# Reordered steps of a block with windowed attention and routed experts: maxima first on VectorE, values behind the scores, the shared expert in the general banks, the second normalisation and what follows it two steps sooner

## The reference

```
x = x + attention(layernorm(x))
x = x + ffn(layernorm(x))
attention: q, k, v = x Wq^T, x Wk^T, x Wv^T; 16 heads of 8 channels; each query sees
           the 64 keys up to itself (blocks of 64, own and previous); softmax; then Wo^T
ffn:       scores = sigmoid(x G) + bias, 16 experts in 4 groups; the 2 groups with the largest
           sum of their top two; in them the top 4 experts, weights normalised times 2.5
           y = sum over experts of weight * (silu(x Wg) * (x Wu)) Wd, experts of width 64
           + silu(x Sg) * (x Su) Sd, a shared expert of width 128
```

## Time and profile before

| | us |
|---|---|
| median of 3 runs (lowest, highest) | 792.83 (791.32, 793.52) |
| profiled execution | 793.12 |
| its span | 791.3 |
| busy: TensorE, weight loads | 699.4, 563.1 |
| busy: VectorE, ScalarE, GpSimd | 507.4, 541.0, 457.4 |

### The profile page before, as it was taken

How to read it: one execution, slowest core, us unless ns; L and a number is a source line. 1 busy time by engine, 2 the same in 40 slices (tenths; PEclk the granted TensorE clock), 3 DMA queues, 4 the chain that set the end, 5 groups by cost and what they waited for, 6 DMA issues and landing times. The chain is left out here.

```text
span 791.3 us, 19511 instructions
## 1 busy us (share of the span) xinstructions
PE 699.4 (88%) x6256; PEld 563.1 (71%) x6256; DVE 507.4 (64%) x1584; ACT 541.0 (68%) x1603; POOL 457.4 (58%) x564
## 2 busy tenths in 40 slices
PE   3566799998989999898989999898999989998887
PEld 2445577777867778686867777777777878786765
DVE  1556666758676665757676675857666576875454
ACT  3586778686877767687776868687776768763232
POOL 5323256657676675757566675767567575435443
PEclk9998799999999999999999999999999999999899
DMA  5000031220303131130403122030313112131321
GB/s 156 1 28 27 1 97 54 80 84 21 123 22 106 53 104 57 47 114 2 133 27 108 53 84 77 21 123 18 109 50 108 53 53 95 38 113 35 101 95 41
DMA packets 50884, 53.63 MB, mean 68 GB/s; under 512 B 5792, under 2 KB 32032, under 8 KB 50720
## 3 DMA queue, kind: packets, MB, share of 16 engines
q1 hardware_dynamic: 50848, 53.18, 21.2%
HBM read 44.25 MB, written 4.72 MB: 62 GB/s over the span
## 5 line engine op out<-in xcount | busy, mean ns | idle before, releaser
L566 ACT ACTIVATE probs<-PS,neg_max 128x96 f32<-128x96 f32 (+1 forms) x1024 | 244.7, 354 | 80.6 <-DVE neg_max L728 80.3
L455 POOL TENSOR_TENSOR gate<-gate,spread 128x512 f32<-128x512 f32 x128 | 163.6, 1278 | 217.7 <-ACT gate L514 105.7
L694 DVE STREAM_TRANSPOSE probsT<-probs 128x768 f32<-128x768 f32 (+1 forms) x128 | 116.3, 908 | 101.6 <-ACT probs L566 101.6
L718 DVE SCALAR_TENSOR_TENSOR tu<-th,PS 128x512 f32<-128x512 f32 x128 | 87.5, 683 | 108.2 <-PE PS L798 77.2
L980 PE MATMUL PS<-wd,hh 128*128 128x128 f32 x1024 | 139.2, 279 | 6.7 <-DVE OUT L708 4.1
L796 PE MATMUL PS<-x_hi,w_hi 128*128 128x512 f32 x288 | 126.9, 441 | 15.3 <-DVE tu L718 14.4
L980 PEld LDWEIGHTS PS<-wd,hh 128*128 128x128 f32 x1024 | 127.3, 193 | 15.2 <-DVE hh L760 5.4
L467 POOL TENSOR_TENSOR hh<-gate,tu 128x512 f32<-128x512 f32 x100 | 128.4, 1284 | 13.7 <-POOL gate L455 13.4
L530 ACT ACTIVATE th<-PS 128x512 f32<-128x512 f32 x128 | 80.2, 627 | 75.7 <-PE PS L798 75.6
L728 DVE TENSOR_REDUCE neg_max<-PS 128x4 f32<-128x384 f32 (+1 forms) x256 | 122.7, 515 | 12.0 <-PE PS L901 10.5
L798 PE MATMUL PS<-x_lo,w_hi 128*128 128x512 f32 x288 | 115.1, 400 | 0.0
(11 more groups left out here) (102 smaller groups left out, 956.0 us busy)
## 6 DMA issues: line engine op xcount, KB each, us to landing
spread<-weights_by_expert SPq DMA_DIRECT2D x256, 128.0 KB, 2.9
X<-x SPq DMA_DIRECT2D x32, 256.0 KB, 3.1
OUT<-H SPq DMA_DIRECT2D x16, 256.0 KB, 2.9
out<-OUT SPq DMA_DIRECT2D x16, 256.0 KB, 3.0
ffn_stage<-w_gu SPq DMA_DIRECT2D x1, 1152.0 KB, 5.7
wd<-w_down SPq DMA_DIRECT2D x1, 512.0 KB, 6.5
weights_by_expert<-cT SPq DMA_DIRECT2D x16, 32.0 KB, 1.6
probsT<-w_att SPq DMA_DIRECT2D x1, 192.0 KB, 3.0
```

The source lines that it names most:

```text
L455: tt(gate2[:, :], gate[:, k % 2, :], spread[:, k % SP_BUFS, :], ALU.mult).then_inc(s_g2, 1)
L566: ins = nc.scalar.activation(probs[:, u % 2, tt, 2 * rows + e, j0:KW], PS[:, rows, n * KW + j0:n * KW + KW], ACT.Exp, bias=neg_max[:, rows ...
L694: v_.transpose(probsT[:, b, :, t0:t0 + 2, c0:3, :].rearrange("p g t c q -> p t g (c q)"), probs[:, u % 2, :, :, c0 * Q:KW]).then_inc(s_pt, 1)
L718: v_.scalar_tensor_tensor(tu[:, k % 2, :], th[:, :], 1.0, PS[:, 5, :], ALU.add, ALU.mult).then_inc(s_tu, 1)
```

## The change

- Stages: VP and VB one step later; LN2 one step sooner, XT2, LG, RT, CT, FF, DN, YE two steps sooner; SH stays in its step.
- The shared expert's gate and up leave banks 4 and 5 for two uses of the ring (LATE, WEIGHTS), with a tanh tile of its own (`th_s`). QP and CT move to the ring's place POST, LG to WEIGHTS, VP to LATE; the ring has 16 uses a slot.
- Within a step TensorE does FF, SC, CT, then PV, OT, ON, OW, SH, QP, KP, VP, LG, DN, XT2, XT. Before, PV, VP and LG came first and DN last.
- VectorE does `tu`, the two maxima, and after them all else; the turning of the probabilities comes late in the step.
- ScalarE does CT's copy and the shared tanh between the two halves of the exponentials, then OE, XT2, LG, XT, QP, KP, VB.
- GpSimd does both expert products first and LN1 last.
- In slots 0 to 2 (`filling`) the two 64-row halves of SC go one after the other, each with its own wait. TensorE starts with 24 tiny matmuls (`WARM`).

```
-QP, KP, VP, VB = 5, 6, 6, 7
+QP, KP, VP, VB = 5, 6, 7, 8
-LN2 = 17
-XT2 = 19
-LG = 24
-RT = 24
-CT = 27
+LN2 = 16
+XT2 = 17
+LG = 22
+RT = 22
+CT = 25
 SH = 27
-FF = 28
+FF = 26
-DN = 29
-YE = 37
+DN = 27
+YE = 35
 RING = (3, 6)
-EARLY, POST, WEIGHTS, LATE = range(4)
+EARLY, POST, LATE, WEIGHTS = range(4)
-    (EARLY, (VP, LG)), (LATE, (XT, QP, KP, XT2, XT2 + 4)),
-    (POST, (OT, OT + 4, ON, ON + 4, OW, OW + 4)), (WEIGHTS, (CT,)))
+    (LATE, (XT, KP, VP, XT2, XT2 + 4, SH)),
+    (POST, (QP, CT, OT, OT + 4, ON, ON + 4, OW, OW + 4)), (WEIGHTS, (LG, SH)))
+def filling(slot):
+    return slot.fixed and slot.n < 3
...
 @block.scalar, in a step
-LG tanh; FF tanh and copy; ON copy; CT copy; SH tanh; XT copy; XT2 copy; SC; QP; KP; OE; VB
+FF tanh and copy; ON copy
+                    for rows in range(2):
+                        if g:
+                            act.wait_ge(s_m, 2 * (g.n * NU + u) + rows + 1)
...
+                            ins.then_inc(s_p, 1)
+                        if rows == 0:
+                            between_halves()      # CT copy, SH tanh
+OE; XT2; LG; XT; QP; KP; VB
...
 @block.vector, in a step
-TR; VP; YE; LN1; tu; routing; SC maxima with routing between; LN2; OT; OW; hh; SH; XT; XT2
+tu; SC maxima; YE; VP; routing; OT; OW; LN2; LN1; TR; XT2; hh; SH; XT
+                        side, bank = filled(dve, sl, s, LATE)
+                        dve.wait_ge(s_ths, g.n + 1)
+                        v_.scalar_tensor_tensor(fa[:, :], th_s[:, :], 1.0, bank, ALU.add, ALU.mult
+                                                ).then_inc(s_taken[side], 1)
+                        taken(dve, sl, s, LATE)
+                        side, bank = filled(dve, sl, s, WEIGHTS)
+                        ins = v_.scalar_tensor_tensor(hs[:, :], fa[:, :], 0.5, bank, ALU.mult, ALU.mult)
+                        ins.then_inc(s_taken[side], 1)
...
 @block.tensor
+            pe.wait_ge(s_pool, 1)
+            for _ in range(WARM):
+                mm(PS[0:NT, 7, 0:NT], half_neg[:, :], half_neg[:, :], start=True, stop=True)
...
+                        if filling(sl):
+                            for rows in range(2):
+                                if not (g.n == 0 and u == 0):
+                                    pe.wait_ge(s_p, 2 * (g.n * NU + u) + rows - 1)
+                                hide(u, rows)
+                                scores(g, u, rows, 0)
+                                scores(g, u, rows, 1)
+                        else:
+                            pe.wait_ge(s_p, 2 * (g.n * NU + u))
+                            hide(u, 0, 1)
+                            for tt in range(2):
+                                for rows in range(2):
+                                    scores(g, u, rows, tt)
...
+                        for place, n in ((LATE, WG), (WEIGHTS, WU)):
+                            side, bank = free(place)
+                            exact3(bank, *w2(n + P * NP), *x2).then_inc(s_filled[side], 1)
```

More of the change, by code:

```diff
@@ L145 @@
 PREPARE = 4
+WARM = 24
 ORDER_PER_SLOT = 5
@@ L721, in slot @@
-                    routing(sl, s, 3)
                     g, u = at(sl, s, SC, 1, NU)
@@ L809, in gate_up @@
                 x2 = x2_hi[:, g.par, :], x2_lo[:, g.par, :]
[L810 to L816 removed]
+                exact3(PS[:, 4, :], *w2(WG + P * k), *x2).then_inc(s_g, 1)
@@ new lines, in gate_up, with hide @@
+                exact3(PS[:, 5, :], *w2(WU + P * k), *x2).then_inc(s_u, 1)
+            def hide(u, *halves):
+                parts = ((0, 2, 1, 1, 1), (2, 4, 0, 2, 1)) if u % 4 == 0 else ((0, 4, 0, 0, 2),)
+                for n0, n1, which, first, step in parts:
+                    for rows in halves:
+                        r = slice(64 * rows, 64 * rows + 64)
+                        dst = PS[:, rows, 0:4 * KW].rearrange("p (n k) -> p n k", n=4)[:, n0:n1, :]
+                        hidden = slice(first, KW // Q, step)
+                        mm(blocks3(dst)[:, :, hidden, :], ident4[r, :],
+                           blocks2(band[r, which, :])[:, hidden, :].unsqueeze(1).broadcast_to(
+                               [64, n1 - n0, len(range(3)[hidden]), Q]),
+                           start=(n0 == 0), stop=False, skip_group_check=True)
@@ L821, in slot, with free @@
                         pe.wait_ge(s_cst, 2)
+                    def free(place):
+                        use = shared_use(sl, s, place)
+                        if not (sl.fixed and use.before == 0):
+                            pe.wait_ge(s_taken[use.bank], use.before)
+                        return use.bank, PS[:, RING[use.bank], :]
+                    g, k = at(sl, s, FF, 1, NP)
+                    if g:
+                        gate_up(g, k)
+                    g, u = at(sl, s, SC, 1, NU)
+                    if g:
+                        if u == 0:
+                            taken(pe, slot_before(sl), QP % STEPS, POST)
+                            taken(pe, slot_before(sl), KP % STEPS, LATE)
+                        if filling(sl):
[11 more added lines that the diff above has]
+                                    scores(g, u, rows, tt)
+                    g, _ = at(sl, s, CT)
+                    if g:
+                        side, bank = free(POST)
+                        pe.wait_ge(s_cb, g.n + 1)
+                        for n in range(NT):
+                            ins = nc.tensor.transpose(bank[0:E, P * n:P * n + P], comb[:, n, :], ident)
+                        ins.then_inc(s_filled[side], 1)
                     for turn_, stage in enumerate(PV):
@@ L844, in slot @@
                             ins.then_inc(s_o_ps, 1)
-                    def free(place):
-                        use = shared_use(sl, s, place)
-                        if not (sl.fixed and use.before == 0):
-                            pe.wait_ge(s_taken[use.bank], use.before)
-                        return use.bank, PS[:, RING[use.bank], :]
-                    g, _ = at(sl, s, VP)
-                    if g:
-                        side, bank = free(EARLY)
-                        exact3(bank, *w2(WV), xT_hi[:, :], xT_lo[:, :]).then_inc(s_filled[side], 1)
```

334 lines of the change are left out of this document (146 added, 188 removed).

## The result

The changed kernel takes 815.73 us (median of 4 runs, 812.19 to 819.33); the kernel before took 792.08 in the same comparison. The ratio is 1.029 [1.025, 1.033]: slower, where 771.2 and "faster" had been predicted. The profiled execution took 816.72 us, its span 814.9.

What follows compares the result with a forecast made beforehand. TensorE was taken as nearest to full in the steady stage (busy 42.39 of 45.20 us a slot). From 793.1 us, fill -12.7, steady stage -3.2 and drain -6 gave 771.2, range 755 to 789.

Steps and rivals of the forecast that it cites:

- Second place, step 6: Steady slot, step 6: TensorE waits for the router's logits behind ScalarE's q, tanh, maxima and product; 2.1 us lost.
- matmuls at half rate inside the steady stage, which would upset every term: Sign of being wrong: TensorE's matmuls at the low clock in the steady slots; no size or chance given.
- the first place: Steady slot, steps 1 to 3: ScalarE's load delays step 2's tanh, so step 3's scores wait for exponentials; 1.0 us lost.
- None for VectorE ahead of the shared expert: Sign of being right: in steady slots TensorE's 1.23 us wait for VectorE goes, the shared expert using other banks.
- Fill: Start through slot 3: shorter score loops and earlier k, less two more expert steps; -12.7 us, bounds -5 and -17.
- The halves: Slots 0 to 2: half-scores wait only for their own exponentials, loop 4.3 to 4.4 us becoming 2.6; priced 8 to 10.
- Slot 3: End of the fill: eight maxima as before, but six steps carry experts, not four; +1.3 us.
- Drain: After the last scores: 18 expert steps remain, not 20, two steps at 3 us; -6, bounds -5 and -9.
- Warm matmuls: Start of the run: 24 tiny matmuls might keep TensorE's rate up; 0 to -3 us, taken as 0.
- A: Rival, steady slot: the waits really go, TensorE stays full at 42.0 to 43 us a slot; 742 us, chance 0.12.
- B: Rival, fill: serial chain limits gain to -5, steady unchanged, drain -5; slots 1, 2 over 31 us; 783 us, chance 0.18.
- C: Rival, steady step 3: VectorE late for the shared expert, next step's output projection waits; 801 us at 4.2 late, chance 0.09.

Runs made afterwards that it cites:

- e1: Changed kernel with six thrown-away 512-column matmuls ahead of the router's logits in step 6 of each slot; 786.35 us, 0.994 of the kernel before.
- e7: Changed kernel with the logits behind the down projection and the k projection ahead of the attention transposes in step 6; 785.18 us, 0.989 of the kernel before.
- e2: Changed kernel with the router's logits behind the down projection in TensorE's order of a step; 780.3 us, 0.988 of the kernel before.
- e8: Kernel of e7 plus three thrown-away 384-column matmuls ahead of each half of the scores in slots 0 to 2; 809.39 us, 1.020 of the kernel before.
- e3: Changed kernel with the halves of the scores in slots 0 to 2 undone; 813.82 us, 1.025 of the kernel before.
- e12: Kernel before the change, with only the scores of slots 0 to 2 split into halves, each with its own wait; 786.45 us, 0.996.
- e13: Kernel of e6 with values ahead of the scores and turning ahead of the maxima in slots 0 to 2; 769.32 us, 0.973 of the kernel before.
- e6: Kernel of e2 plus two thrown-away matmuls ahead of step 6's attention transposes and two ahead of the logits; 771.27 us, 0.973 of the kernel before.
- e4: Changed kernel with the value products ahead of the scores again everywhere, turning still behind the maxima; 982.93 us, 1.241 of the kernel before.
- e11: Kernel of e6 without the 24 early tiny matmuls (WARM = 0); 778.45 us, 0.983 of the kernel before.
- e10: Kernel of e6 with VectorE turning the probabilities at the start of its step in all slots; 774.15 us, 0.980 of the kernel before.
- e5: Kernel before the change, with step 6's k projection in slots 4 to 15 made to wait for VectorE's divided attention output; 831.84 us, 1.049.

## Why the prediction was wrong, point by point

**Steady slot: the step that failed is "Second place, step 6 ... Lost: 2.1 us".** The wait was right: 0.59 + 1.44 = 2.03 us, for the reason given (q, the copy, tanh, tu, the maxima, the product, in this order). The earlier trace rows come back in the new trace (q from 405.20 to 407.6, tanh from 407.47), VectorE from tu to the product:

```profile
408.13 0.69 DVE L710 SCALAR_TENSOR_TENSOR tu<-th,PS 128x512 f32<-128x512 f32 x1 [2.37 <-ACT th L531]
408.74 1.01 DVE L718 TENSOR_REDUCE neg_max<-PS 128x4 f32<-128x384 f32 x2
410.05 0.42 DVE L741 TENSOR_TENSOR o_n<-PS,o_rs 128x256 f32<-128x256 f32 x1
```

Its price was wrong. I priced a wait of TensorE at its length. This one also cost the clock behind it, 2.7 us a slot by e1, more than its own length. Without the fall the slot is 44.5 us where 44.9 were predicted, and with it 47.2 in the mean. Of the stage's 27.4 us of error, then, the clock is 31.9, and the rest of the estimate erred by 4.5 to the safe side, some 0.4 a slot. I had named "matmuls at half rate inside the steady stage, which would upset every term" among the signs of being wrong, but gave it no chance and no price. A row to do it with was there: the earlier trace rows have a clock of 0.94 in a tail with waits. Against it stood a wait of 1.23 us in each steady slot without a fall. I took the 1.00 of the steady stage as given; it belonged to that order of the work, and not to the length of its gaps alone: waits no longer (1.17 in e7, 0.60 and 0.55 in e2) came with falls.

TensorE: Matmul & The Clock Gate (Part 1) of the Trainium skill, which the prediction had weighed for the warm matmuls alone, says that activity lifts the clock and idleness takes it back. The windows of step 6 agree: 0.89 busy of 2.30 us, then 0.50. It should have been weighed at each wait that the change adds. The fill of e8 does not agree: TensorE busy for 30.2 us, and the rate stayed low. There the measurement decides.

**Steady slot, the first place (1.0 us).** Measured: 0.44 us in the mean for the exponentials. I had more than twice that, in the cautious direction. "None for VectorE ahead of the shared expert" holds. A slip in the sum: the eight steps that I listed add up to 41.3 us, not 41.5.

**Fill (-12.7, measured +8.3).** The first maxima are right (-1.5 for -1.9), and for the reason given: ScalarE spreads k directly behind q, from 15.30, where it was 17.12; the wait of 1.30 us for q's bank is still there, now ahead of the v projection. The halves were sized at 8 to 10 us and are worth 2.6 in this order (e3) and at most 5.7 in the old one (e12). I had laid slots out as if the scores' loop were the only one; two other chains came into it. The timelines of TensorE and VectorE in the first step of slot 2 show one of them:

```profile
50.08 2.83 PE L909 MATMUL PS<-probsT,v_bd 128*64 128x96 f32 x32
52.84 0.87 PE L939 MATMUL PS<-wo,oT 128*128 128x128 f32 x4
```

```profile
50.19 0.42 DVE L718 TENSOR_REDUCE neg_max<-PS 128x4 f32<-128x256 f32 x1 [0.54 <-PE PS L844]
...
53.75 0.42 DVE L751 TENSOR_TENSOR H<-PS,X 128x256 f32<-128x256 f32 x1 [3.14 <-PE PS L939]
...
55.76 0.98 DVE L718 TENSOR_REDUCE neg_max<-PS 128x4 f32<-128x384 f32 x2
```

The values (2.83 us at the low clock) and the output projection now stand behind the scores; VectorE waits 3.14 us for them, and behind its residual addition and the turning come the next maxima, at 55.76. The step takes 6.5 us; it took 3.3 before. In e13 it takes 2.9 again. The second is at step 6: the attention transposes wait for q, and the logits come behind at the low clock.

```profile
79.11 0.66 PE L922 MATMUL PS<-cst,o_f 128*128 128x128 f32 x4 [2.13 <-ACT q_by_head L520]
```

That is the wait of the steady stage's second place. I had it in the steady slot and left it out of the fill. By its length it is hardly new: the kernel before waits 1.96 us at the same transposes, for ScalarE's copy of the attention output. The logits behind it take 2.7 us, from 80.68 to the next scores at the low rate; in the kernel before they take 1.4 us, at full rate (85.19, ahead of slot 3's first scores). With the old order of values and turning the fill is still 69.2 us (e13), 7.4 over the old order with halves (e12, 61.8). What these 7.4 us are is open. What moved two steps sooner and the wait for q are candidates. So is the clock: slots 1 and 2 have 38 us at 1.2 GHz in e13 and 19 in e12, and at the steady stage's 1.6 to 1.7 us per 3.4 the 19 us more are, as an estimate, worth up to 9. The same holds for the 38 and 30 us of the changed kernel and the one before. I have no run that parts them.

**Slot 3 (+1.3, measured +5.7).** Two more expert steps explain a part: e13 and e6, which have them and neither the steady gap nor its price, take 44.1 and 44.9, 2.9 and 3.7 over the 41.2 before. The rest up to 46.8 fits the same gap and clock; no run tests it by itself.

**Drain (-6, measured -8.9).** Direction right; it reached my outer bound of -9. No run tests the mechanism, the two steps fewer. The clock has a part in it: in the tail it is at 1.2 GHz for 11.0 us before and for 7.4 after, which by the same price is, as an estimate, 1.7 of the 8.9 us.

**Warm matmuls (0).** Nothing gained is shown, as taken: the v projection runs at half rate with them in the changed kernel, at full rate with them in e4 and without them in e11, and slots 1 and 2 take the same with and without them (71.6 and 71.7). That the run without them is 7 us longer comes from elsewhere.

**The rivals.** A is refuted: the waits came. B's sign is there in slot 2 alone (40.8 us; slot 1 took 30.8, under its 31), but B had no loss in it, and the fill lost. C, the one slower case, had the wrong place: no wait of the output projection for VectorE's step 3 appears. The mechanism that decided stood in none of them, so all numbers of the range were on its wrong side.

**The sum again**: 771.2 predicted; +21.0 up to the end of slot 3, +27.4 in the steady stage, -2.9 in the drain make the 816.7 measured, to 0.1.

## What to carry to other kernels

A wait of TensorE has two prices, its length and the clock that it may cost behind it; where the steady stage stands at 1.00, every gap that an edit adds must be priced with it (waits of 0.6 to 2.2 us carried it here, some of them every time). A gap that must stay can be filled with thrown-away matmuls that end before the operand is there (29 us here), better still shortened first and then filled (44 us); in the fill, where the path runs through TensorE's short steps, fillers only lengthened it. Moves on two engines that share data (who turns, who uses what was turned) are to be priced together: values first without turning first cost 167 us (e4), turning first alone cost nothing to speak of (e10).

## What the runs showed of the hardware that was not expected

- The clock fell to 1.2 GHz each steady slot behind waits of 0.59 and 1.44 us in a slot where TensorE was otherwise busy all the time, and it fell after the work had resumed, 0.7 to 1.1 us after in ten slots (410.5 and 411.6 in one of them) and 2.7 us after in two. It stayed down for 3.4 or 6.8 us, each 3.4 costing 1.6 to 1.7 us.
- It is not a sharp rule of length. A wait of 2.2 us in the kernel before (e5) came with a fall in six of twelve slots; 1.17 (e7) in nine; 0.60 and 0.55 (e2) in five; 1.23 (before) in none. The orders of the work around the waits differ.
- At the start of a run the granted clock can't be taken at its word. Its record begins with an entry of full clock (36.2 us before, 36.1 in the changed kernel, 47.2 in e8, 14.3 in e11); ahead of it the windows read 1.00, while the matmuls have the durations of 1.2 GHz.
- Being busy did not lift it there: in e8 TensorE is busy all the time from 17.0 to 47.2, at the low rate. The first rise comes between 14.2 and 47.2 us in these runs; the 24 early matmuls do not decide it (e4 has them and rises at 14.2, e11 has none and rises at 14.3).
- Removing 24 instructions ahead of the loops (e11) went with waits of up to 1.58 us on "issue", once at each new turn of the loop, 6.2 us in all. It stays open why.
